# A GRU scan on one core: the prologue with x first and W_hh's last part in two pieces, and the input products spread over steps 246 to 253

## The reference

```python
x = x + conv(x, cond[:, None, :])            # depthwise, causal, K = 16 taps
def cell(h, x):
    gi = x @ W_ih + b_ih
    gh = h @ W_hh + b_hh                     # each [16, 1536]: r, z, n
    r = sigmoid(i_r + h_r); z = sigmoid(i_z + h_z)
    n = tanh(i_n + r * h_n)
    return (1 - z) * n + z * h
x = x + scan(cell, cond, x)
```

## Time and profile before

| | us |
|---|---|
| median of 3 runs (1026.89 to 1027.08) | 1027.0 |
| the profiled execution, its own time | 1026.88 |
| its span, first to last instruction | 1025.1 |
| TensorE busy | 1014.5 (99%) |
| VectorE busy | 865.6 (84%) |
| ScalarE busy | 399.4 (39%) |
| GpSimd busy | 237.7 (23%) |

### The profile page before, as it was taken

How to read it: one execution, slowest core, us unless ns; L and a number is a source line. 1 busy time by engine, 2 the same in 40 slices (tenths; PEclk the granted TensorE clock), 3 DMA queues, 4 the chain that set the end, 5 groups by cost and what they waited for, 6 DMA issues and landing times.

```text
span 1025.1 us, 58209 instructions
## 1 busy us (share of the span) xinstructions
PE 1014.5 (99%) x24837; PEld 935.8 (91%) x24838; DVE 865.6 (84%) x2850; ACT 399.4 (39%) x1816; POOL 237.7 (23%) x784
## 2 busy tenths in 40 slices
PE   8999999999999999999999999999999999999997
PEld 5987777777999999999999999999999999999996
DVE  7788888888888888888888898888888877777554
ACT  5334333343433334343333434333343433334342
POOL 3222222222222222222222222222222222222222
PEclk9999999999999999999999999999999999999999
DMA  8721000010100101001010010101001000000000
GB/s 296 73 34 39 19 21 30 15 36 19 31 23 15 32 19 34 24 11 35 15 39 19 15 36 11 39 19 29 26 11 35 14 29 18 9 29 4 25 14 12
DMA packets 66450, 32.07 MB, mean 31 GB/s; under 512 B 43920, under 2 KB 65040, under 8 KB 66192
## 3 DMA queue, kind: packets, MB, share of 16 engines
q1 hardware_dynamic: 65760, 28.25, 10.8%
q10 hardware_dynamic: 432, 0.11, 0.0%
HBM read 19.86 MB, written 8.49 MB: 28 GB/s over the span
## 4 chain that ended last, share of the span: by engine, by line
PE 97%; issue 2%; POOL 1%; DVE 0%; DMA 0%; ACT 0%; POOLq 0%; DVEq 0%
PE pg L307 65%; PE pg L297 32%; POOL tz L259 1%; PE pcv L335 0%; DMA cnd<-cond 0%; DVE hp L542 0%; DVE gn L521 0%; POOL nzh L272 0%; DVE gt L517 0%; POOLq L44 0%; POOL cpad L251 0%; ACT rz L439 0%; DVE an L529 0%; POOL cpad L249 0%; POOL nzh L256 0%
## 5 line engine op out<-in xcount | busy, mean ns | idle before, releaser
L307 PE MATMUL pg<-whh,hp 128*32 128x192 f32 x16368 | 717.8, 326 | 4.2 <-DVE hp L542 2.8
L307 PEld LDWEIGHTS pg<-whh,hp 128*32 128x32 f32 x16368 | 616.7, 110 | 53.9 <-issue 4.7
L297 PE MATMUL pg<-wih,x 128*32 128x192 f32 x8192 | 386.4, 326 | 0.0
L272 POOL TENSOR_TENSOR nzh<-rz,hp 128x32 f32<-128x32 f32 x512 | 158.1, 309 | 782.0 <-ACT rz L439 782.0
L297 PEld LDWEIGHTS pg<-wih,x 128*32 128x32 f32 x8192 | 307.5, 110 | 24.0
L439 ACT ACTIVATE rz<-gt 128x64 f32<-128x64 f32 x512 | 136.8, 267 | 484.6 <-DVE gt L517 460.8
L484 DVE SCALAR_TENSOR_TENSOR x<-xb,cnd,x 128x512 f32<-128x512 f32 (+1 forms) x420 | 295.1, 703 | 8.0
L542 DVE TENSOR_TENSOR_SCAN hp<-zcp,nzh 128x96 f32<-128x96 f32 x512 | 173.7, 339 | 41.8 <-ACT nzh L444 41.5
L517 DVE STREAM_TRANSPOSE gt<-pg 128x128 f32<-128x128 f32 x512 | 160.5, 314 | 50.6 <-PE pg L307 43.8
L529 DVE TENSOR_TENSOR_SCAN an<-rz,gn 128x64 f32<-128x64 f32 x512 | 149.2, 291 | 52.3 <-ACT rz L439 51.8
L444 ACT ACTIVATE nzh<-an 128x32 f32<-128x32 f32 x512 | 120.8, 236 | 126.8 <-DVE an L529 126.8
(11 more groups left out here) (45 smaller groups left out, 46.8 us busy)
## 6 DMA issues: line engine op xcount, KB each, us to landing
xb<-x SPq DMA_DIRECT2D x96, 94.0 KB, 2.0
out<-x SPq DMA_DIRECT2D x60, 128.0 KB, 1.9
wih<-w_ih SPq DMA_DIRECT2D x4, 768.0 KB, 7.9
whh<-w_hh SPq DMA_DIRECT2D x4, 768.0 KB, 14.5
xw<-x SPq DMA_DIRECT2D x24, 64.0 KB, 3.5
xb<-x SPq DMA_DIRECT2D x16, 62.0 KB, 1.9
tz<-taps SPq DMA_DIRECT2D x12, 64.0 KB, 3.4
xs<-x SPq DMA_DIRECT2D x1, 512.0 KB, 4.6
```

The source lines that it names most:

```text
L272: pool.tensor_tensor(nzh[:, f, ::2, :, 1], chunks(rz[:, f, 1, :, 1]), h_of(t - 1, slice(f * CH, (f + 1) * CH)), ALU.mult).then_inc(s_zh[f], 1)
L297: i = pe.matmul(pg[m % Q][f][D * j:D * (j + 1), RZ:END], x1_of(c, 2 * m, 2 * m + 2), wih[:, c, :, :].rearrange("p (g k) (j d) -> p j g k d ...
L307: i = pe.matmul(pg[t // 2 % Q][f][D * j:D * (j + 1), 0:IN], hp[:, t % 2, 2 * c + 1 - t % 2:2 * c + 3 - t % 2, :, 1].rearrange("p u b -> p ...
```

## The change

The semaphores: `s_whl` for the second piece of W_hh part 3, `s_seed_n` and `s_gn` for a bank `pcv[1]` that takes step 0's h products for n, `s_last` for the last addition of half 1.

- The load of cond moves from SP's queue to the head of ScalarE's, so xs is SP's first. W_hh part 3 is loaded in two pieces, r and z (512 KB), then n (256 KB).
- Step 0's products for n go to `pcv[1]`, seeded with their biases, straight from the loaded columns (`recur_n`), apart from r and z (`recur_rz`), so they no longer wait for ScalarE's copies. For part 3 all r and z stand ahead of all n; VectorE's `transpose_n(0, f)` waits for `s_gn`.
- `product` takes a running number q. Pair 2's part 3 products stand in the place of some fillers (`IDLE` 5 and 3 become 3 and 4), and one more behind part 2; step 1 has three groups in place of four. From step 246 to 253 each step has three groups.
- `LATE` goes from 22 to 18. The input transposes of pairs 126 and 127 move: half 1 of pair 126 from step 250 to 251, pair 127 from steps 251 and 252 to 252 and 253. The wait for `s_tin[1]` stands behind `recur(t, 0, 1)`.
- The last output addition is done in two halves, GpSimd half 0 and VectorE half 1.

```diff
-LATE = 22
-IDLE = {0: 5, 1: 3}
+LATE = 18
+IDLE = {0: 3, 1: 4}
+THIN = 245
...
+        def products(t):
+            def until(t):
+                n = C * (t + 1) if t <= THIN else C * (THIN + 1) + (C - 1) * (t - THIN)
+                return 2 * H * C + min(n, H * C * (M2 - 2))
+            return range(until(t - 1) + (t == 1), until(t))
+        def inputs(t):
+            if t == 0:
+                return range(2, 4)
+            if t < T - 6:
+                return range(t + 3, t + 4)
+            return range(t + 2, min(t + 3, T)) if t > T - 6 else range(0)
...
-            sp.dma_start(cnd[:, :, :], cond).then_inc(s_cnd, 16)
             sp.dma_start(xs[:, :, :], x[:, :, 0:TB * B]).then_inc(s_xs, 16)
...
-            for c in range(C):
+            for c in range(C - 1):
                 sp.dma_start(whh[:, c, F:], w_hh[:, c, :]).then_inc(s_whh[c], 16)
+            sp.dma_start(whh[:, C - 1, F:3 * F], w_hh[:, C - 1, 0:2 * F]).then_inc(s_whh[C - 1], 16)
+            sp.dma_start(whh[:, C - 1, 3 * F:], w_hh[:, C - 1, 2 * F:]).then_inc(s_whl, 16)
...
-            add_out(T - 1)
+            pool.wait_ge(s_h[0], T + 1)
+            o = x1_of(slice(0, CH), T - 1, T)
+            pool.tensor_tensor(o, o, h_of(T - 1, slice(0, CH)), ALU.add).then_inc(s_o, 1)
...
-            def product(m, f, c):
+            def product(q):
+                m, f, c = q // (H * C), q // C % H, q % C
+                if m == 2:
+                    c = (c - 1) % C
...
+            def recur_n(f, c):
+                for j in range(J):
+                    i = pe.matmul(pcv[1][D * j:D * (j + 1), f * RZ:(f + 1) * RZ],
+                                  hp[:, 0, 2 * c + 1:2 * c + 3, :, 1].rearrange("p u b -> p (u b)"),
                                   whh[:, c, 3 * F:].rearrange("p (j f n) -> p j f n", j=J, f=H)[:, j, f],
                                   start=False, stop=True, skip_group_check=True)
...
-            for c in range(C):
+            pe.wait_ge(s_seed_n, H)
+            for c in range(C - 1):
                 pe.wait_ge(s_whh[c], 16)
-                if c < C - 1:
-                    pe.wait_ge(s_whn, c + 1)
                 for f in range(H):
-                    if c < C - 1:
-                        recur(0, f, c)
-                    else:
-                        recur_first(f, c).then_inc(s_gh[f], 1)
+                    recur_rz(f, c)
+                    recur_n(f, c)
+                if c < H:
+                    product((2 * H + c) * C)
                 for _ in range(IDLE.get(c, 0)):
                     pe.matmul(pcv[0][:, :], zeros[:, 0:P], zeros[:, :], start=True, stop=True)
-            for c in range(C):
-                product(2, 0, c)
+            product(2 * H * C + 1)
+            pe.wait_ge(s_whh[C - 1], 16)
+            for f in range(H):
+                recur_rz(f, C - 1).then_inc(s_gh[f], 1)
+            pe.wait_ge(s_whl, 16)
+            recur_n(0, C - 1)
+            recur_n(1, C - 1).then_inc(s_gn, 1)
+            for c in range(1, C - 1):
+                product(2 * H * C + c + 1)
...
                 if t % 2 == 0:
                     pe.wait_ge(s_tin[0], m + 1)
-                    pe.wait_ge(s_tin[1], m + 1)
                 pe.wait_ge(s_h[0], t + 1)
                 recur(t, 0, 0)
                 recur(t, 0, 1)
+                if t % 2 == 0:
+                    pe.wait_ge(s_tin[1], m + 1)
                 recur(t, 1, 0)
...
-                    if m + 2 < M2:
-                        product(m + 2, t % 2, c)
+                    for q in products(t)[c:c + 1]:
+                        product(q)
...
+            act.dma_start(cnd[:, :, :], cond).then_inc(s_cnd, 16)
...
+            for f in range(H):
+                act.activation(pcv[1][:, f * RZ:(f + 1) * RZ], bc[:, f, 0:RZ], ACT.Copy).then_inc(s_seed_n, 1)
...
             for c in range(C):
-                act.wait_ge(s_whh[c], 16)
+                act.wait_ge(s_whh[c] if c < C - 1 else s_whl, 16)
...
+                if t == 0:
+                    dve.wait_ge(s_gn, 1)
+                g = pg[t // 2 % Q][f][:, 0:RZ] if t else pcv[1][:, f * RZ:(f + 1) * RZ]
...
-                if t == 0:
-                    transpose_in(1, 0)
-                m = (t + 1) // 2 + 1
-                if m < M2:
-                    transpose_in(m, 1 - t % 2)
+                for i in inputs(t):
+                    transpose_in(i // H, i % H)
...
+            dve.wait_ge(s_h[1], T + 1)
+            o = x1_of(slice(CH, C), T - 1, T)
+            dve.tensor_tensor(o, o, h_of(T - 1, slice(CH, C)), ALU.add).then_inc(s_last, 1)
```

More of the change, by code:

```diff
@@ L90, in build @@
         s_whh = [sem(f"s_whh{c}") for c in range(C)]
+        s_whl = sem("s_whl")
         s_whn = sem("s_whn")
@@ L113, in build @@
         s_x1 = sem("s_x1")
+        s_seed_n = sem("s_seed_n")
         s_seed = halves("s_seed")
@@ L116, in build @@
         s_tin = halves("s_tin")
+        s_gn = sem("s_gn")
         s_gh = halves("s_gh")
@@ L126, in build @@
         s_o = sem("s_o")
+        s_last = sem("s_last")
         block = ctx.enter_context(nc.Block())
@@ L235, in _ @@
             sp.wait_ge(s_o, b)
+            sp.wait_ge(s_last, 1)
             sp.dma_start(out[:, :, a * B:b * B], x1_of(slice(None), a, b)).then_inc(s_out[len(STORES) - 1], 16)
@@ L286, in product @@
                     pe.wait_ge(s_first, len(FIRST))
+                if q % C == 0:
+                    pe.wait_ge(s_seed[f], m + 1)
                 if c == 0:
-                    pe.wait_ge(s_seed[f], m + 1)
                     if FEW <= 2 * m < TB:
@@ L300, in product @@
                                   start=False, stop=True, skip_group_check=True)
-                if c == C - 1:
+                if q % C == C - 1:
                     i.then_inc(s_gi[f], 1)
@@ L311, in recur, with recur_rz @@
                 return i
-            def recur_first(f, c):
-                hh = hp[:, 0, 2 * c + 1:2 * c + 3, :, 1].rearrange("p u b -> p (u b)")
+            def recur_rz(f, c):
                 for j in range(J):
-                    o = pg[0][f][D * j:D * (j + 1), :]
-                    pe.matmul(o[:, RZ:IN], hh,
-                              whh[:, c, F:3 * F].rearrange("p (g j f n) -> p j f g n", g=2, j=J, f=H)[:, j, f],
-                              start=False, stop=True, skip_group_check=True)
-                    i = pe.matmul(o[:, 0:RZ], hh,
+                    i = pe.matmul(pg[0][f][D * j:D * (j + 1), RZ:IN],
+                                  hp[:, 0, 2 * c + 1:2 * c + 3, :, 1].rearrange("p u b -> p (u b)"),
+                                  whh[:, c, F:3 * F].rearrange("p (g j f n) -> p j f g n", g=2, j=J, f=H)[:, j, f],
+                                  start=False, stop=True, skip_group_check=True)
+                return i
+            def recur_n(f, c):
+                for j in range(J):
+                    i = pe.matmul(pcv[1][D * j:D * (j + 1), f * RZ:(f + 1) * RZ],
+                                  hp[:, 0, 2 * c + 1:2 * c + 3, :, 1].rearrange("p u b -> p (u b)"),
                                   whh[:, c, 3 * F:].rearrange("p (j f n) -> p j f n", j=J, f=H)[:, j, f],
@@ L349, in _ @@
                     pe.matmul(pg[q][f][:, :], zeros[:, 0:P], zeros[:, :], start=True, stop=True).then_inc(s_bits, 1)
+            pe.matmul(pcv[1][:, :], zeros[:, 0:P], zeros[:, :], start=True, stop=True).then_inc(s_bits, 1)
             for _ in range(WARM):
@@ L363, in _ @@
                     for f in range(H):
-                        product(m, f, c)
+                        product((m * H + f) * C + c)
             pe.wait_ge(s_tin[0], 1)
@@ L410, in seed @@
                 if m < Q:
-                    act.wait_ge(s_bits, 2 * Q)
+                    act.wait_ge(s_bits, 2 * Q + 1)
                     act.wait_ge(s_bc, H)
@@ L520, in transpose_n @@
             def transpose_n(t, f):
+                if t == 0:
+                    dve.wait_ge(s_gn, 1)
+                g = pg[t // 2 % Q][f][:, 0:RZ] if t else pcv[1][:, f * RZ:(f + 1) * RZ]
                 dve.transpose(gn[:, t // 2 % 2, :, f, :, :, 0].rearrange("p u c b -> p c u b"),
-                              pg[t // 2 % Q][f][:, 0:RZ]).then_inc(s_tn[f], 1)
+                              g).then_inc(s_tn[f], 1)
             def scan_n(t, f):
```

## The result

The changed kernel takes 1030.4 us (median of 6 runs, 1030.01 to 1032.35), the kernel before 1026.86 beside it: 1.0038 times as long, with a 95% interval of 1.0028 to 1.0048. I had forecast 1024.6, 2.3 faster; it is 3.5 slower. The profiled execution is the longest of the six, 1032.35 by its own clock. SP is SyncE, the engine that issues the large loads here, and PSUM is the memory that TensorE's matmuls write.

A forecast was written before the change was run, and what follows sets the result against it. TensorE's own row count was taken to bound steps 2 to 251, with waits only at both ends. Tail 1.45, prologue 0.4, step 1 0.2 and end 0.2 sum to 2.25: 1026.88 to 1024.6 us; range over all 1023.8 to 1025.8.

The forecast's parts named there:

- the one on loads: Prologue: xs first brings the loads 0.42 us forward; cond, even 0.7 us later, is covered by TensorE's wait until 17.71.
- rival 5: Even steps mid-run: the wait for half 1's input transpose breaks TensorE's stream; at 50 ns each, 1031; chance 0.03.
- I am wrong if the granted clock leaves 2.4 GHz: Failure sign: clock falling between the shorter fillers and step 1, where TensorE idles some 0.9 us.
- TensorE's row from part 0 to step 1: Prologue: TensorE starts part 0 at about 17.1 and step 1 at 24.45; prologue gain 0.4 us.
- everything behind follows: I take 0.42: Prologue: xs issued 0.45 us earlier on SP brings all loads behind it 0.42 earlier, between 0 and 0.45.
- rival 2: Prologue gives nothing: loads don't move or TensorE's chain is 0.4 longer; 1025.0; chance 0.09.
- rival 1: Prologue bound by the loads alone, gaining 0.8 us; 1024.2; chance 0.14.
- Rival 4: Split of W_hh's last part costs a fixed 1.84 us for the second piece; 1025.2; chance 0.02.
- The tail: Steps 246 to 253 run at the gate chain's pitch, 29.28 us instead of 30.72; gain 1.45, bounds 0.7 to 1.84.
- the spare of 0.12: Tail: h of half 1 is done at 1011.07, 0.12 us before TensorE wants it at 1011.19.
- Rival 3: Tail: pitch with products is longer, 3.75 us, as late half 1 h delays the next chain; 1025.4; chance 0.12.
- Step 1 and the end: Step 1 loses a product group, 3.70 instead of 3.90 us; VectorE adds the last half 1; gain 0.2 each.

The follow-up runs named there:

- experiment 8: Against experiment 6: SP issues x first and cond second, leaving the biases alone at the head of ScalarE's queue; 1025.64 us, ratio 0.9987.
- Experiment 4: Kernel before with only cond's load moved from the head of SP's queue to the head of ScalarE's; 1028.76 us, ratio 1.0023.
- experiment 1: Changed kernel with cond's load back at the head of SP's queue; 1025.33 us, ratio 0.9984.
- experiment 2: Changed kernel with 18 more matmuls on zeros ahead of step 0, keeping TensorE busy in the gap; 1029.02 us, ratio 1.0019.
- experiment 9: Changed kernel again, unedited, for a second profile; 1030.44 us, ratio 1.0037.
- experiment 3: Kernel before with only the tail, the moved transposes and waits and the split last addition; 1025.52 us, ratio 0.9985.
- experiment 6: Changed kernel with cond back first on SP's queue, LATE 22 and fillers 2 and 2; 1024.66 us, ratio 0.9977.
- 7: Against experiment 6: GpSimd instead of ScalarE copies the n columns of W_hh's last part; 1024.69 us, ratio 0.9978.
- experiment 5: Changed kernel with both biases ahead of cond on ScalarE's queue, SP still starting with x; 1031.2 us, ratio 1.0037.

## Why the prediction was wrong

**The step that failed** is the one on loads: "cond goes to ScalarE's queue and may now be later ... it is covered". I priced the move for the load that is moved and not for the two that it is put ahead of. cond was in fact on time: 1.78 us to landing, and its readers were not late. But `bih` and `bhh` slipped from first and second place on that queue to second and third. Before, `bhh` was issued at 1.25, landed in 1.7 us, and VectorE's bias copies, behind the wait for cond in its order, found it there. Now it lands at 8.27. Its place on the queue isn't all of it: x now goes first, and with x first `bhh` takes 3.7 even in its old second place (experiment 8). VectorE takes its work in order, so the wait stops the convolution, which the prediction itself had as the chain to the input transposes. Experiment 4, this edit alone, shows the slip; experiment 1, all but this edit, shows it gone. The forecast read SP's queue and never ScalarE's, and it took VectorE's start from the wait for x without asking what stands in VectorE's order ahead of it. None of my five rivals had it; rival 5 put the slower side in the middle of the run instead.

**The size.** Late biases make part 0 start at 21.0 to 21.2 instead of 17.42, and step 1 3.8 us late (experiments 1 and 2). The low clock adds 1.3 to 2.5 (experiments 2 and 9). By the medians, 3.7 lie between experiments 1 and 2 (1025.33 and 1029.02) and 1.4 between experiment 2 and the changed kernel (1030.4), together 5.1.

**The clock.** "I am wrong if the granted clock leaves 2.4 GHz" came true, though in front of part 0, where TensorE idled 4.0 us, and not where I looked. The Trainium skill, page "TensorE: Matmul & The Clock Gate", section "Part 1: The HAM clock gate", says that the clock depends on how busy TensorE has been recently; the trace agrees, 0.50 after 4.0 us of no matmul and 1.00 where fillers take their place. The 1.43 us before part 0, which the prediction took as its safe case, had become the 4.0.

**The prologue's own terms.** TensorE's row from part 0 to step 1 was forecast at 7.35 and is 7.42 and 7.44 (experiments 1 and 2). But "everything behind follows: I take 0.42" was mis-sized: the copy that follows the landing of W_hh's last piece starts at 22.22 in the changed kernel's profile and at 22.05 in experiment 9, against 22.38, so 0.16 to 0.33 earlier. That is no more than such a landing scatters: in experiment 3, whose loads are those of before, the copy starts at 22.73. Over the profiles whose W_ih isn't held back it starts at 22.21 to 22.73 with x second (before, experiments 1, 3, 6; GpSimd's in 7) and at 22.05 to 22.41 with x first (changed kernel, 2, 4, 8, 9), some 0.2 earlier in the mean; but in experiment 5, also x first, it starts at 21.08, and no run says why. Experiments 6 and 8, x second and x first, differ by 0.07 in the other direction. In experiment 1, with cond ahead of x, the transposes stood at 16.95 (the forecast, with x first, was 16.6) and the gain is 0.02. No run has x first with both the biases and cond early, so the 0.42 stays untested by itself. That is rival 2, nothing from the prologue, for the filler and `LATE` settings of the change; with those of experiment 6 it is rival 1, 0.70 against its 0.8.

**The split of W_hh's last part.** Rival 4, a fixed time for the second piece, is false: in experiment 6 the gate rows start at 21.59 and the n piece is there at 22.21, the whole part's time of before less 0.17. A wait of 1.84 behind the gates' landing would show. The premise, that cond's 1.84 us are those of "a lone load", was loose as well: `bih` was in flight on ScalarE's queue and x behind it.

**The tail.** 1.45 forecast, 1.33 measured, and 1.30 alone in experiment 3. Pitches are 3.59, 3.71, 3.61, 3.85, 3.60, 3.71, 3.61 and 3.71. The eight steps took the chain's pitch as forecast, but for step 249, whose 64 rows take 2.95 instead of 2.81: h of half 1 is ready at 1002.19 and the forecast's slack, 0.98 after 1001.13, ended at 1002.11. That is the spare of 0.12, used up. The row names ScalarE's tanh for the late scan, which had ended 0.2 before, so what is behind it stays open. But it isn't new: all 13 profiles have it, that of the kernel before too, where the same scan of step 248 reads

```profile
995.31 0.36 DVE L542 TENSOR_TENSOR_SCAN hp<-zcp,nzh 128x96 f32<-128x96 f32 x1 [0.36 <-ACT nzh L444]
```

and starts 0.23 behind the end of the tanh (994.84 + 0.24), as in steps 36 and 224; in the other 253 steps that gap is 0.07 or less there. There TensorE's longer steps hid it: the h is ready at 995.67 and wanted at 994.90 + 0.98 = 995.88. The forecast took its spare of 0.12 from one step, 252, and didn't look at the steps that were to become bound by the chain. Rival 3, 3.75 throughout, is false; rival 5 too, since steps 2 to 245 take 954.43 in experiments 1 and 9, with the wait in mid-step, as they did before.

**Step 1 and the end** came as forecast, 0.20 and 0.19. The last addition in the changed kernel:

```profile
1027.32 0.36 DVE L589 TENSOR_TENSOR_SCAN hp<-zcp,nzh 128x96 f32<-128x96 f32 x1 [0.30 <-POOL x L301]
1027.72 0.19 DVE L644 TENSOR_TENSOR x<-x,hp 128x32 f32<-128x32 f32 x1
```

It starts 0.04 behind the scan and takes 0.19, where GpSimd took 0.14 and 0.32.

**Why the third small load is the late one** can be read in part from the DMA records of the changed kernel, here from 4.75 to 7.75 us (q1 is SP's queue, q10 ScalarE's; packets, MB, share of the 16 engines):

```profile
DMA packets 343, 1.06 MB, mean 354 GB/s; under 512 B 160, under 2 KB 173, under 8 KB 343
q1 hardware_dynamic: 191, 1.05, 92.6%
q10 hardware_dynamic: 152, 0.01, 3.8%
```

The 6 KB of `bhh` are small in bytes but move as 128 packets of 48 bytes. All 128 lie in this stretch, single ones between 170 packets of W_ih of 6144 bytes, which last 0.234 us each at the median. That is 8 small packets for each of the 16 engines and, by estimate, 8 x 0.234 = 1.9 us if each waits for one large packet. `bih`'s 128 packets run from 2.99 to 4.41 between x's packets of 1024 bytes, 0.046 us each. In the kernel before, all 256 packets of both biases are through by 2.57, before x's begin. The Trainium skill, page "DMA: Bandwidth & Descriptors", section "Queues, rings and completion order", says that each DMA engine turns between the queues that have work, a packet at a time. The counts agree with that, though these records don't give the engine of a packet. What stays open is the first half of the wait: `bhh`'s first packet comes 3.1 us after its issue, 0.4 behind `bih`'s last one.

## What to carry to other kernels

When a load moves to the head of another queue, price every load that it now stands before, and follow each to the engine that waits for it: VectorE's in-order wait for 6 KB of biases cost more than all that the edit could give. Count a load's packets as well as its bytes, and the large packets that they will have to pass. Once a stretch gets a wait of some microseconds on TensorE, count the clock as well. And fillers set for one landing time become the bound when landings move; set them again, as experiment 6 did. A spare that is read from one step holds for that step; read it in each step that is to depend on it.
